# Row-frequency convolution kernel: the forward transform as 128x32 float32 matmuls, and row weights that contract real and imaginary parts together

## The reference

```python
# layer 1: x = x + conv(gn(x)), the convolution is done on the spectrum
X = jnp.fft.rfftn(x, axes=(-2, -1))
Xr, Xi = jnp.real(X), jnp.imag(X)
Yr = _rconv(Xr, wr) - _rconv(Xi, wi) + b_real      # 3x3, 16 -> 16 channels
Yi = _rconv(Xr, wi) + _rconv(Xi, wr) + b_imag
y = jnp.fft.irfftn(lax.complex(Yr, Yi), axes=(-2, -1))
```

## Time and profile before

| | |
|---|---|
| median of 3 runs | 6231.96 us (6223.27 to 6234.69) |
| the profiled execution | 6232.09 us, its span 6230.2 us |
| PE busy | 5335.2 us (86%) |
| DVE busy | 5053.6 us (81%) |
| ACT busy | 4538.9 us (73%) |
| POOL busy | 3153.6 us (51%) |
| mean granted PE clock | 0.949 of full speed |

### The profile page before, as it was taken

One profiled execution on the slowest core, in us unless ns is written; L12 is line 12 of the kernel. 1 busy time (PEld: TensorE's weight loads), 2 busy tenths in 40 slices (PEclk: granted clock), 3 DMA queues, 4 the chain that ended last, 5 costly groups with the idle time before them and its releaser, 6 DMA issues. The chain is left out here.

```text
span 6230.2 us, 202732 instructions
## 1 busy us (share of the span) xinstructions
PE 5335.2 (86%) x63882; PEld 3402.6 (55%) x63882; DVE 5053.6 (81%) x10660; ACT 4538.9 (73%) x8793; POOL 3153.6 (51%) x5676
## 2 busy tenths in 40 slices
PE   0379979979979979979989989968898988989889
PEld 0058748748748748747757757833343433434334
DVE  5879979979979989988998998986676766767664
ACT  2578768868868867867876666768787877878775
POOL 3178768758858858858857858921111110111102
PEclk9889989989989989999999999989999999999999
DMA  6516616616616625625624524646676766767665
GB/s 203 158 47 209 204 40 206 207 46 201 206 53 190 208 69 171 208 88 159 206 95 115 159 84 113 177 94 155 166 204 163 204 162 159 200 162 196 168 163 139
DMA packets 535621, 958.88 MB, mean 154 GB/s; under 512 B 121946, under 2 KB 126938, under 8 KB 532826
## 3 DMA queue, kind: packets, MB, share of 16 engines
q1 hardware_dynamic: 467546, 798.95, 45.0%
q10 hardware_dynamic: 67456, 151.01, 7.8%
HBM read 560.40 MB, written 287.60 MB: 136 GB/s over the span
## 5 line engine op out<-in xcount | busy, mean ns | idle before, releaser
L1655 PE MATMUL pC<-xs,taps 128*128 128x512 f16 x4608 | 1095.8, 383 | 106.7 <-DMA xhalo<-xs 100.4
L981 PE MATMUL pM<-gw,xh 64*128 64x256 f16 (+1 forms) x24960 | 1130.7, 244 | 5.5 <-DVE yt L1141 4.7
L981 PEld LDWEIGHTS pM<-gw,xh 64*128 64x128 f16 x24960 | 972.5, 95 | 133.4 <-issue 12.0
L1551 POOL TENSOR_TENSOR xn<-xn,one_col 128x1 f32<-128x1 f32 x520 | 170.4, 328 | 1406.4 <-ACT xn L1585 1406.4
L1655 PEld LDWEIGHTS pC<-xs,taps 128*128 128x128 f16 x4608 | 449.3, 98 | 672.1 <-DVE xs L1705 90.2
L1571 ACT ACTIVATE scaled<-X,qbias,qscale 128x512 f32 (+1 forms) x512 | 413.3, 808 | 327.8 <-DMA X<-after_layer 297.0
L742 POOL TENSOR_TENSOR X<-X,zo 128x256 f32 (+1 forms) x512 | 372.5, 727 | 548.3 <-DVE zo L1105 548.3
L279 PE MATMUL pM<-X,mix0s 64*64 64x512 f32 x2304 | 530.1, 634 | 134.5 <-DVE X L1073 108.5
L723 POOL TENSOR_TENSOR X<-X,rl 128x512 f32 x384 | 478.4, 1275 | 270.8 <-ACT rl L772 270.7
L1593 ACT ACTIVATE xs<-xn 128x1028 f16<-128x1028 f32 x520 | 546.8, 1051 | 86.7 <-POOL xn L1552 86.2
L1712 DVE SCALAR_TENSOR_TENSOR result<-pC,X 128x512 f32<-128x512 f32 x512 | 352.4, 688 | 303.3 <-DMA out_dram<-result 181.4
(11 more groups left out here) (249 smaller groups left out, 13574.2 us busy)
## 6 DMA issues: line engine op xcount, KB each, us to landing
gw<-row_weights SPq DMA_DIRECT2D x520, 288.0 KB, 3.4
after_layer<-X SPq DMA_DIRECT2D x512, 256.0 KB
out_dram<-result SPq DMA_DIRECT2D x512, 256.0 KB
X<-in_x_dram SPq DMA_DIRECT2D x448, 256.0 KB
X<-after_layer ACTq DMA_DIRECT2D x224, 512.0 KB, 5.7
stage<-in_x_dram SPq DMA_DIRECT2D x192, 512.0 KB
xhalo<-xs SPq DMA_DIRECT2D x504, 96.4 KB, 3.7
qhalo<-q SPq DMA_DIRECT2D x496, 96.2 KB, 3.9
```

What stands on the lines that cost most here:

```text
L981: nc.tensor.matmul(pY[:, r, col:col + nd * P], row(xh, r)[:, k, p, ri, off:off + P], weights(r, q_, d, nd, ri), start=ri == 0 and off == 1 ...
L1655: nc.tensor.matmul(bank, taps3[:, d, wh], xs[:, h, own, d:d + W], start=d == 0 and n == 0, stop=False)
```

## The change

The forward transform loses its split into float16 halves. `xt` is kept in float32, the tables too, and the product is one float32 matmul with a stationary operand of 128x32 (two bands) that writes 32 partitions of PSUM. Four of them, for both halves r and for the real and imaginary part, fill the four quarters of `pF`'s partitions; so the partitions of `pF`, and with it of `xh`, hold the real and the imaginary parts of two bands side by side, and the column half (`a`, the pass) says which two bands. The low half of `xt` on DVE is gone.

The row weights are rebuilt for that: one contraction over 64 partitions now sums over the real and the imaginary part of two bands, and gives 32 columns for each output block where it gave 64. `gw`, `gbuf` and the DRAM table shrink from 1152 to 768 float16 values per partition and item. In the set-up, `comp` has four pieces of 96 in place of two of 144.

```diff
@@ tables and sizes
-GB = 3 * HP
-GW = 2 * 3 * GB
+PASSES = 2
+QB = HB // PASSES
+QP = HP // PASSES
+GX = 6
+GB = GX * QP
+GW = PASSES * 2 * GB
@@ set-up, DVE
-                                for t in range(2):
+                                for t in range(2 * PASSES):
@@ set-up, ACT
-                            for s in range(HB):
+                            for s in range(QB):
@@ set-up, POOL
                             for t in range(2):
-                                m = spread_lo(n % 3, n % 2, t)
+                                for a in range(PASSES):
+                                    m = spread_lo(n % 3, n % 2, t, a)
@@ ACT, step
-                            nc.scalar.activation(xt[:, k, 0], pT[:, :], ACT.Copy).then_inc(xt_hi, 1)
+                            nc.scalar.activation(xt[:, k], pT[:, :], ACT.Copy).then_inc(xt_in, 1)
@@ PE, step, forward
-                            for n in range(2):
-                                three(pF[:, 0, n * NO:(n + 1) * NO], lambda h, c=n + 2: xt[:, o, h, c * P:(c + 1) * P],
-                                      lambda h, n=n: fwd_odd[:, n, h], n == 0, n == 1)
-                            three(pF[:, 1, 0:NO + 2], lambda h: xt[:, o, h, 0:P], lambda h: fwd_0[:, 0, h], True, False)
-                            m = three(pF[:, 1, NO + 2:2 * NO + 4], lambda h: xt[:, o, h, P:2 * P], lambda h: fwd_2[:, 0, h], False, True)
+                            def forward(a, chunk, table, bank, col, n):
+                                for r in range(2):
+                                    for part in range(2):
+                                        row, band = r * HP + part * QP, r * HP + a * QP
+                                        c = chunk(part) * P + band
+                                        m = nc.tensor.matmul(pF[row:row + QP, bank, col:col + n], xt[:, o, c:c + QP], table(part),
+                                                             start=True, stop=True)
+                                return m
+                            for a in range(PASSES):
+                                forward(a, lambda part: 2 + part, lambda part: fwd_odd[:, part], 0, a * NO, NO)
+                                forward(a, lambda part: 0, lambda part: fwd_0[:, part * (NO // 2 + 1):(part + 1) * (NO // 2 + 1)],
+                                        1, a * (NO // 2 + 1), NO // 2 + 1)
+                                m = forward(a, lambda part: 1, lambda part: fwd_2[:, part * (NO // 2 + 1):(part + 1) * (NO // 2 + 1)],
+                                            1, NO + 2 + a * (NO // 2 + 1), NO // 2 + 1)
@@ PE, step, row weights
-                            for ri in range(2):
-                                for off, d, nd, col in ((1 + NO, 0, 2, 0), (1, 1, 2, 0), (0, 0, 1, P), (2 + NO, 2, 1, 0)):
+                            for a in range(PASSES):
+                                for off, d, nd, n0 in ((1 + NO, 0, 2, 0), (1, 1, 2, 0), (0, 0, 1, 2), (2 + NO, 2, 1, 0)):
                                     for n, (p, q_) in enumerate(((0, 0), (0, 1), (1, 0))):
                                         for r in range(2):
-                                            nc.tensor.matmul(pY[:, r, col:col + nd * P], row(xh, r)[:, k, p, ri, off:off + P],
-                                                             weights(r, q_, d, nd, ri),
+                                            nc.tensor.matmul(out(a, r)[:, n0:n0 + 2 * nd], row(xh, r)[:, k, p, a, off:off + P],
+                                                             row(gw, r)[:, s, a, q_, d:d + nd].rearrange("p d (c m) -> p (d c) m", m=QP),
@@ DVE, step
-                        if on(0):
-                            dve.wait_ge(xt_hi, q + i + 1)
-                            nc.vector.tensor_tensor(xt[:, k, 1], pT[:, :], xt[:, k, 0], ALU.subtract).then_inc(xt_lo, 1)
```

More of the change, by code:

```diff
@@ L62, in tables @@
     t["bandmask"] = (s1[:, None] == np.arange(BANDS)[None, :]).astype(np.float32)
-    phi = 2 * np.pi * (J * s1[:, None] + np.arange(J)[None, :]) / H
-    t["trig"] = np.stack([np.ones_like(phi), np.cos(phi), np.sin(phi)], -1).astype(np.float32)
+    rowhalf, part, sub = p // HP, p % HP // QP, p % QP // C
+    own = rowhalf[:, None] * HB + np.arange(PASSES)[None, :] * QB + sub[:, None]
+    phi = 2 * np.pi * (J * own[:, None, :] + np.arange(J)[None, :, None]) / H
+    t["trig"] = np.stack([np.cos(phi), np.sin(phi)], -1).astype(np.float32)
+    t["part_mask"] = (part[:, None] == np.arange(2)[None, :]).astype(np.float32)
+    t["sub_band"] = (sub[:, None] == np.arange(QB)[None, :]).astype(np.float32)
+    rows = 2 * np.pi * (J * s1[:, None] + np.arange(J)[None, :]) / H
+    waves = np.stack([np.ones_like(rows), np.cos(rows), np.sin(rows)], -1)
     sums = np.zeros((P, J, HB, C), np.float32)
-    sums[p, :, 0:3, c1] = t["trig"]
+    sums[p, :, 0:3, c1] = waves
     t["sumw"] = sums.reshape(P, J, HP)
@@ L81, in fwd @@
         m[np.abs(m) < 1e-9] = 0
-        return np.stack(halves(m), 2).transpose(1, 0, 2, 3).copy()
+        return np.ascontiguousarray(m[0]).astype(np.float32)
     t["fwd_0"] = fwd(4 * np.arange(NO // 2 + 1), P)
@@ L89, in tables @@
     m[np.abs(m) < 1e-9] = 0
-    t["fwd_odd"] = np.stack(halves(m), 2)
+    t["fwd_odd"] = m.astype(np.float32)
     n2 = np.arange(HALF)
@@ L447, in _, with by_part @@
                             put(ws, k, src, sign)
+                        def by_part(dst, src):
+                            link(nc.vector.tensor_scalar(dst, src[:, :, 1:3], part_mask[:, 0:1], None, ALU.mult))
+                            link(nc.vector.scalar_tensor_tensor(out=dst, in0=src[:, :, 0:2], scalar=part_mask[:, 1:2], in1=dst,
+                                                                op0=ALU.mult, op1=ALU.add))
+                        for n, v in enumerate((base, wc, ws)):
+                            by_part(own[:, n], v)
                         dve.sem_inc(masks_ready, 1)
-                        flat = [v[:, :].rearrange("p a b o -> p (a b o)") for v in (base, wc, ws)]
+                        flat = [own[:, n].rearrange("p a b o -> p (a b o)") for n in range(3)]
                         def moments(j):
@@ L979, in step @@
+                            for a in range(PASSES):
+                                for off, d, nd, n0 in ((1 + NO, 0, 2, 0), (1, 1, 2, 0), (0, 0, 1, 2), (2 + NO, 2, 1, 0)):
                                     for n, (p, q_) in enumerate(((0, 0), (0, 1), (1, 0))):
                                         for r in range(2):
-                                            nc.tensor.matmul(pY[:, r, col:col + nd * P], row(xh, r)[:, k, p, ri, off:off + P],
-                                                             weights(r, q_, d, nd, ri),
-                                                             start=ri == 0 and off == 1 + NO and n == 0,
-                                                             stop=ri == 1 and off == 2 + NO and n == 2)
@@ L986, in step @@
-                            for t, (ri, a, d, blk) in enumerate(((0, NO, 0, 1), (1, NO, 0, 0), (0, NO + NE, 1, 1))):
-                                for n, (p, q_) in enumerate(((0, 0), (0, 1), (1, 0))):
-                                    for r in range(2):
-                                        m = nc.tensor.matmul(pY[0:1, r, P + HP:2 * P], row(xh, r)[:, k, p, ri, a:a + 1],
-                                                             row(gw, r)[:, s, q_, d, blk * HP:(blk + 1) * HP], start=t == 0 and n == 0, stop=t == 2 and n == 2)
+                                            nc.tensor.matmul(out(a, r)[:, n0:n0 + 2 * nd], row(xh, r)[:, k, p, a, off:off + P],
+                                                             row(gw, r)[:, s, a, q_, d:d + nd].rearrange("p d (c m) -> p (d c) m", m=QP),
+                                                             start=a == 0 and off == 1 + NO and n == 0,
+                                                             stop=a == 1 and off == 2 + NO and n == 2)
@@ new lines, in step @@
+                            for a in range(PASSES):
+                                for t, (col, d) in enumerate(((NO, 0), (NO + NE, 1))):
+                                    for n, (p, q_) in enumerate(((0, 0), (0, 1), (1, 0))):
+                                        for r in range(2):
+                                            m = nc.tensor.matmul(out(a, r)[0:1, 3], row(xh, r)[:, k, p, a, col:col + 1],
+                                                                 row(gw, r)[:, s, a, q_, d, 0:QP], start=a == 0 and t == 0 and n == 0, stop=a == 1 and t == 1 and n == 2)
```

95 lines of the change are left out of this document (50 added, 45 removed).

## The result

The change makes the kernel faster by 0.8%, a fifth of what was forecast: 6183.83 us (6163.93 to 6191.85, 4 runs) against 6232.22 us (6223.27 to 6234.69, 4 runs), a ratio of 0.992 with a 95% interval of 0.9903 to 0.9937. The forecast was 5990 us, 5935 to 6130. The profiled execution of after took 6191.85 us, 40 less than that of before; its span is 6189.9 us.

The account below looks back on a forecast made before the run. PE was taken to bound the spectral stage, with DVE close behind. From 6232 us, 171 (steps with pairs), 50 (steps without) and 20 (set-up) came off, giving 5991, stated as 5990 us, range 5935 to 6130.

Parts of the forecast that it names:

- The pace of PE: Spectral stage: PE's step falls by 0.52 us, to 4.35 without a pair and 4.93 in the mean with pairs.
- rivals 1 and 2: 1: Forward's four tile streams don't run at once, 6380 us, 10%; 2: weight loads limit PE, 6115 or 6165 us, 14%.
- The change part by part, per step on PE: Spectral stage, PE's step: forward +0.37, row weights -0.95, edge +0.06 us, costed by columns and changes of shape.
- the 221 forecast: Gain in the spectral stages: 171 us from steps with pairs and 50 us from steps without.
- Rival 3: Spectral stage: the chain PE, ACT, DVE through the single buffers holds PE up, 6082 us, 14%.
- PE's clock: Sign of a wrong forecast: a PE clock under 1.00 within the spectral stage.
- The set-up: Before the spectral stages: smaller row-weight stores save 31 us, less DVE's added work; 20 us taken, from -4 to 31.

Follow-up runs that it names:

- e1: After without the streamed 512 KB transfers of the image after next: 6021.61 us.
- e4: Before with each row-weight matmul split in two of half the columns, so more PE instructions: 6553.3 us.
- e3: After with forward, row-weight and edge matmuls merged into fewer, wider ones, 198 PE instructions a step for 278: 5974.37 us.
- e6: After with the edge matmuls of high times high alone, 8 in place of 24, so 32 PE instructions a step fewer: 5982.18 us.
- e11: Before without the streamed transfers of the image after next, the control for e1: 6226.71 us.
- e2: After with ACT's two sums over the streamed rows cut to 8 columns, all transfers kept: 6190.05 us.
- e8: After with each 1 MB set-up chunk of image 0 loaded in eight transfers of one band: 6153.36 us, ratio 0.9873.
- e9: Before with the same band-wise set-up loads of image 0 as e8: 6177.82 us.
- e7: After with each streamed 512 KB transfer issued as eight transfers of one band: 6543.0 us.
- e5: After with streamed rows sent singly in each step, not two every second step, and band-wise set-up loads of image 0: 6152.93 us.

## Why the prediction was wrong

**The pace of PE: right.** The forward part was to be 1.05 us to the first row-weight matmul and is 1.03; the row weights 1.13 and are 1.13; the edge 0.42 and is 0.38; the step without a pair 4.35 and is 4.34; with pairs 4.93 in the mean and is 4.87. Four 128x32 tiles do run at once, and the 64-column pairs are not held up by their loads. So rivals 1 and 2 are out. DVE without its subtraction and POOL with its 4.42 us stand as forecast: e1 runs at DVE 95%.

**What failed** is the step "The change part by part, per step on PE". It costs a matmul by its columns and by changes of shape, "and 0.04 us for its 12 records", and takes instructions as free. The text notes that "4 matmuls of 512 columns are 8 records", and never adds up what that makes: 48 records in place of 12 in the forward part, 24 for 18 at the edge, 278 instructions for 194 in a step that is to be shorter by a tenth. The supply of instructions is in no term, no rival and no bound. Measured, this term is 247 us of excess in images 0 to 6: without it the stages would have given 33.5 + 247 - 4 = 276 us (4 is before's own excess). These 276 are more than the 221 forecast: with pairs 0.11 us a step over 364 steps, 40 us, from a mean of 4.87 for 4.98 with its 0.05 for waits; and in the first twelve steps of images 0 to 6, for which the forecast took POOL as the pace, 39 us for the 25 forecast (63 steps at 0.40 us). What the runs put in its place: stalls appear in before when only instructions are added (e4), go or shrink when they are taken out of after (e3, e6), stand at multiples of 256 instructions, and for the larger part need the traffic (e1), which costs nothing where blocks last 6.8 us (e11).

**Rival 3**, the chain through the single buffers, forecast 6082 us with the wrong cause. e2 takes nearly a fifth of ACT's work in the window away, to no effect, and PE has no stop of over 1 us in after that is not at a border. The rows that would have spoken for it (`DVE xh <- ACT xh`, 23.7 us) are what PE's stalls leave behind.

**PE's clock** was to show the error if under 1.00; it was 0.96 in this window, where PE stands still again and again, and 1.00 in e1, where it hardly does. The granted clock falls at or behind some of the stops: in step 26 of image 0 PE stops from 548.3 to 551.0, and from 552.1 to 555.5 the clock is at its lower level, 1.2 GHz. That step takes 9.68 us for 5.40; 2.7 of the 4.3 us more are the stop, 1.6 the slow stretch. In after 18.2 us an image lie at the lower level in these steps, none in before. At half speed that is up to 9 us, an estimate, of the excess of 39.6, beside 28.3 us of stops of over 0.5 us at borders. So a part of the excess is an echo of the stalls, by way of the clock.

**The set-up: wrong, small.** 20 us were forecast, from 31 by bytes less DVE's part; it came to -4. The step that failed is "the stores lose a third, 6.3 MB, or 31 us at that rate": a store took as long with a third less in it. What it waited for was its place behind 1 MB loads. e8 changes only how these are cut, and a store lands in 5.8 us. "DMA: Bandwidth & Descriptors" of the Trainium skill, section "Why a DMA increments its semaphore by 16 and not by 1", has the reason: the number of engines that a transfer uses is the largest up to 16 that divides the slowest dimension of both access patterns. For the chunks that is 8 (bands), for a band's own load 16 (channels). The drop from 14.2 to 5.8 us agrees, and so does the mean share of the 16 engines at 10 to 20 us, 0.57 in after and 1.03 in e8; which single engines were busy no view here shows. The rate rose little there, from 140 to 154 GB/s. DVE's added work, forecast at 32 us and hidden behind the stores, goes with some 10 us once they no longer hide it (e8 against e9).

On the refills "Runtime: NRT & Kernel Launch" of the Trainium skill, section "Instruction fetch mechanics", says that an engine's instructions come in blocks of 16 KiB while the current ones run, and that the cost of crossing a border is mostly hidden. The first half agrees with the packets and the multiples of 256. The second holds for before, with 0.7 us of excess an image, and not for after, with 39.6.

**Still open:** why e4 stalls twice as much as e6 with blocks of the same length. Its refills land later (8% of them over 5 us after the start of the block, 1% in e6). It moves half as much again of `gw`, but that was not tried alone. And whether a refill waits in line behind data on one DMA engine, or is asked for late: e7 was meant to tell and did not. A refill's packet itself takes 0.9 to 1.7 us in all of after, and the one of 507.60 starts only at 506.61, so what is late is its start.

## What to carry to other kernels

Count instructions as well as columns: a float32 matmul is two loads and two matmuls, and narrow tiles multiply both. In unlooped code with DMA traffic beside it, see how long 256 PE instructions last: 6.8 us hid nearly every refill here, and 4.3 to 4.7 us cost 17 to 40 us in each stage of some 310 to 385. In a profile, "issue" waits of 2 to 3 us in the middle of a group of matmuls, while all other engines wait for PE or one another, are the sign; look for the instruction packets of that moment, and count PE's instructions from stop to stop. Smaller bursts of data beside them help too: single rows in place of pairs halved the stops (e5), though there other waits took the gain. And where small transfers land late beside large loads, cut the loads another way before making the small ones smaller: 14.2 us became 5.8 by that, and 14.4 stayed 14.2 by a third fewer bytes.

## What was new of the hardware

Late refills are not spread at random. From landing to landing of PE's 16,384-byte packets, worked out from the trace's records of packets (image 1, steps 13 to 63, means over every eighth interval, in us):

```
after   4.5  4.8  4.4  4.2  6.2  6.6  4.2  4.3
e1      4.5  4.4  4.3  4.4  5.4  5.0  4.0  4.0
e6      4.0  3.8  5.7  3.8  5.6  4.2  7.4  5.3
```

In after and e1 two neighbours of eight are late, in after at the same places in nearly every image: steps 18, 26, 32, 39, 46 or 47, 54 and 62, so 6 to 8 steps apart, where 8 blocks last 7.1 steps. Eight packets are 128 KiB, and by the section "Instruction fetch mechanics" of "Runtime: NRT & Kernel Launch" of the Trainium skill this is the size of PE's instruction memory, so it may be the turn of its ring; no run here tested that. In e6, with 8 blocks nearly equal to 8 steps, the late one comes in steps 12, 20, 28, 36, 44, 52 and 60 of image 1. Where a kernel can't have fewer instructions, it might at least have its slack at these places; this was not tried.
